# Eight GpSimd scatters moved two steps later in each turn of a selective-scan stage

## What is computed

```python
x = x + mamba(layernorm(x))      # per prompt: in_proj, conv, silu, delta, B, u
    # dA = exp(delta * -(n+1)), dBu = delta * u * B_n, 16 states n, 512 channels
    # h[t] = dA[t] * h[t-1] + dBu[t];  y[t] = sum_n h[t];  gate, out_proj
# routing of each prompt of the result:
e, p = top_k(softmax(layernorm(x) @ Wr), 2)
buf[e, b, pos] += x_rep          # every token is sent to its two experts' slots
```

## Time and profile before

| | |
|---|---|
| median of three runs | 3001.99 us (2996.59 to 3004.52) |
| profiled execution, its own time | 3004.03 us |
| its span, first to last instruction | 3002.2 us |
| mean granted TensorE clock | 0.968 |
| state-space stage, last scan begins | at 1601.8 us |
| a turn, from `last_send` to `last_send` (turns 3 to 15) | 97.2 to 98.1 us |
| the eight sends of a prompt, first to last start, turn 8 | 733.2 to 758.3 us |

### The profile page before, as it was taken

How to read it: one execution, slowest core, us unless ns; L and a number is a source line. 1 busy time by engine, 2 the same in 40 slices (tenths; PEclk the granted TensorE clock), 3 DMA queues, 4 the chain that set the end, 5 groups by cost and what they waited for, 6 DMA issues and landing times. The chain is left out here.

```text
span 3002.2 us, 48292 instructions
## 1 busy us (share of the span) xinstructions
PE 2777.6 (93%) x16944; PEld 2232.6 (74%) x16944; DVE 2243.1 (75%) x3482; ACT 1754.1 (58%) x3175; POOL 2216.2 (74%) x1565
## 2 busy tenths in 40 slices
PE   7899999999999999999976999999898986999998
PEld 3566666666566666666666999999777776999998
DVE  4999999989999999989886565656465554656564
ACT  5776777667766777677754454444445443545443
POOL 4889999999999999999996676664254446666664
PEclk9999999999999999999988999999999997999999
DMA  6222321132212321122122455553222223555552
GB/s 175 97 89 73 102 91 56 63 96 94 71 54 87 102 88 44 59 87 77 57 66 95 111 135 119 126 121 74 58 83 74 70 88 109 124 123 125 120 122 36
DMA packets 184204, 273.19 MB, mean 91 GB/s; under 512 B 35687, under 2 KB 156174, under 8 KB 175816
## 3 DMA queue, kind: packets, MB, share of 16 engines
q1 hardware_dynamic: 148680, 227.92, 24.1%
q0 software_dynamic: 35328, 42.76, 8.0%
HBM read 188.89 MB, written 94.72 MB: 94 GB/s over the span
## 5 line engine op out<-in xcount | busy, mean ns | idle before, releaser
L570 POOL TENSOR_TENSOR dbu<-du,bb 128x1024 f32<-128x1024 f32 x512 | 1195.8, 2362 | 21.9 <-DVE hs L730 16.6
L730 DVE TENSOR_TENSOR_SCAN hs<-da,dbu 128x1024 f32<-128x1024 f32 x512 | 1152.6, 2279 | 76.2 <-ACT da L665 34.5
L665 ACT ACTIVATE da<-delta 128x512 f32<-128x512 f32 x1024 | 568.1, 594 | 228.2 <-DVE hs L730 225.4
L835 PEld LDWEIGHTS yT<-ident,hs 128*128 128x128 f32 x4096 | 486.9, 146 | 138.0 <-issue 97.1
L835 PE MATMUL yT<-ident,hs 128*128 128x128 f32 x4096 | 543.8, 283 | 10.4 <-DVE hs L730 10.4
L1464 POOL TENSOR_TENSOR ffn_w_lo<-ffn_w,ffn_w_hi 128x512 fp32r<-128x512 f32 x240 | 319.9, 1350 | 78.0 <-ACT ffn_w_hi L1459 76.2
L1550 PE MATMUL ffn_hbank<-ffn_w_hi,ffn_hT_hi 128*128 128x256 f32 x1280 | 366.9, 287 | 1.6 <-DVE ffn_hT_lo L1537 1.6
L1552 PE MATMUL ffn_hbank<-ffn_w_hi,ffn_hT_lo 128*128 128x256 f32 x1280 | 361.2, 282 | 0.0
L1551 PE MATMUL ffn_hbank<-ffn_w_lo,ffn_hT_hi 128*128 128x256 f32 x1280 | 360.5, 282 | 0.0
L1515 PE MATMUL ffn_hbank<-ffn_rowsT_hi,ffn_w_hi 128*128 128x320 f32 x1024 | 318.6, 311 | 4.0 <-POOL ffn_w_lo L1464 3.3
L1516 PE MATMUL ffn_hbank<-ffn_rowsT_lo,ffn_w_hi 128*128 128x320 f32 x1024 | 318.1, 311 | 0.0
(11 more groups left out here) (279 smaller groups left out, 4966.4 us busy)
## 6 DMA issues: line engine op xcount, KB each, us to landing
bb<-b_rows SPq DMA_DIRECT2D x64, 1024.0 KB, 4.7
ffn_w<-L_ffn_W SPq DMA_DIRECT2D x60, 1024.0 KB, 8.8
slots<-empty SPq DMA_DIRECT2D x40, 530.0 KB, 7.4
empty<-slots SPq DMA_DIRECT2D x16, 662.5 KB, 5.0
ffn_rows<-slots SPq DMA_DIRECT2D x16, 662.5 KB, 4.9
xt<-L_attn_a_x SPq DMA_DIRECT2D x16, 512.0 KB
a_xn<-L_attn_a_x SPq DMA_DIRECT2D x16, 512.0 KB, 3.8
x_after_mamba<-a_xn SPq DMA_DIRECT2D x16, 512.0 KB
```

Of the source, the lines that this page charges most:

```text
L570: pool.tensor_tensor(dbu[:, s % DEEP], du[:, dt, :].unsqueeze(1).to_broadcast([P, SN, T]), bb[:, q * SN:(q + 1) * SN, :], ALU.mult).then_i ...
L665: ins = act.activation(da[:, s % 2, i, :], delta[:, par, dt, :], ACT.Exp, scale=-float(q * SN + i + 1))
L730: dve.tensor_tensor_scan(flat[0], flat[1], flat[2], 0.0, ALU.mult, ALU.add).then_inc(scanned.sem, 1)
L835: mm = pe.matmul(yT[:, j * P:(j + 1) * P], hs[:, s % DEEP, i, j * P:(j + 1) * P], k.ident[:], start=False, stop=(q == QS - 1 and i == SN - ...
```

## The change

The sends go behind the products of steps 3 to 10, where they stood behind those of steps 1 to 8. Nothing else is changed, and the lists of TensorE, VectorE, ScalarE and the DMA queue of SyncE are the same.

```diff
                     for s in range(STEPS):
                         if has_main(turn):
                             input_step(pool, turn - 1, s)
-                        if 1 <= s < 1 + NT * K and has_late(turn - 1):
-                            route_send(pool, r, turn - 3, s - 1)
+                        if 3 <= s < 3 + NT * K and has_late(turn - 1):
+                            route_send(pool, r, turn - 3, s - 3)
```

## The result

The changed kernel takes 3063.9 us (median of four runs, 3059.9 to 3069.6) where the kernel before, run beside it, takes 3002.2 us (2996.6 to 3004.5). The ratio is 1.0198, interval 1.0168 to 1.0228: 61.8 us slower. The forecast was 3064.8 us, range 3034 to 3090, and slower by over 0.3%.

The account below looks back on a forecast made before the run. Bound: TensorE's full stretch from 735.0 to 799 us and ScalarE's behind it. 41.8 us (holds net of order) plus 21 (clock) on 3004.0 gives 3066.8, less 2.0 for the median: 3064.8 us, range 3034 to 3090.

Parts of the forecast that it names:

- The order: GpSimd's later sends end TensorE's waits for hx (8.4 us in 13 turns) and turn 16's two waits: 11.0 us less.
- Turn 16's term: In turn 16, where TensorE isn't full, two waits of 1.28 us go whole: 2.6 us less.
- VectorE's wait for dbu at step 9: VectorE's scan of step 9 waits 1.29 us for GpSimd's product; this wait was to go.
- The holds: GpSimd's products of steps 2 and 3 delay VectorE's L262 to L269, so the first scan: 41.8 us net of the order.
- How the operations are held: L262, L264, L269 on VectorE each wait for a GpSimd product's end; the first scan starts 4.17 us later.
- The clock: TensorE's clock falls behind the new gap ahead of its full stretch: 1.5 us a turn, 21 us; bounds 0 and 47.
- No collision: Rival: VectorE's small operations get in between GpSimd's products, only the order counts: -11.0 us, 2991 us; chance 0.09.
- One product only: Rival: VectorE's chain runs through behind product 2: +9.3 us, with some lost clock 3010 to 3020 us; chance 0.07.
- The delay taken up by the wait for ysb: Rival: TensorE's later wait for ysb shrinks by 3.1 us a turn, so nothing is lost: about 3000 us; chance 0.03.

Follow-up runs that it names:

- run 1: The changed kernel, with GpSimd waiting for r_done ahead of the product of step 2: 2935.6 us, ratio 0.9965 to the kernel before.
- run 5: The changed kernel, with TensorE repeating its four uD matmuls seven times more ahead of step 0 in turns 3 to 16: 2988.5 us, ratio 1.0141 to the kernel before.
- run 4: The changed kernel without any edit, on a chip of the experiments: 3012.1 us, ratio 1.0224 to the kernel before.
- run 2: The changed kernel, with the sends behind the products of steps 2 to 9: 2980.7 us, ratio 1.0120 to the kernel before.

## Why the prediction was right

- **The order, −11.0 us.** Right in its sum, and run 1 alone measures it (−11.0). By that run's trace, against that of before from the first chip, turns 3 to 15 are 9.6 us shorter, where 8.4 was forecast, and turn 16 is 0.6 us shorter, where 2.6 was forecast, so the agreement to a tenth is luck. Turn 16's term failed because VectorE's waits there did not go whole: those for dbu fall from 2.6 us to 1.3 in run 1 and to nothing in the changed kernel, but those for da grow from 0.4 to 1.5 and 2.1. One step in the working was wrong as well: VectorE's wait for dbu at step 9 was to go, and in run 1 it only moves to step 11.
- **The holds, 41.8 us.** TensorE's new waits are 47.7 us in 13 turns and 3.96 in turn 16. Less the 8.4 for hx and the 2.6 forecast for turn 16 that is 40.7, and run 5, where the delay stands alone, gives 41.9 (40.1 by its stage). The first scan was to be 4.17 us late and TensorE 3.77: it waits 3.2 to 4.0.
- **How the operations are held.** The forecast had L262, L264 and L269 wait for the ends of products 1, 2 and 3, or L262 and L264 for those of 2 and 3. Seven turns go the first way and three the second. In four L262 is held for two products, which the forecast hadn't. The end is the same product, so no term changes. The port lock that the Trainium skill describes (SBUF — State Buffer, section Who interferes with whom) fits the rows of the change: copies and operations with two SBUF inputs are held (L262, L264 and L269: 0.36, 2.40 and 2.31 us), the scans with da in PSUM keep their 2.29 us. No run shows why a waiting L262 is sometimes passed over for a second product.
- **The clock, 21 us.** What is left of the stage's 66.0 us is 25.3, of which 5.7 stands in the two waits for uD, for which the forecast had no term; run 5 against run 4, which were made on two chips, gives 23.6. The value taken was 2.6 to 4.3 us short, within its bounds of 0 and 47. The value was picked between wide bounds because the gap is about as long as those of the other turns, and that reason doesn't hold: run 2 has as much of the loss with half the gap. That it came out close is in part luck.
- **The rivals.** No collision: excluded by the earlier trace rows against the chain of 5.6 us after. One product only: excluded in the change, and where it was made so (run 2) it costs 34 us, not the 8 to 18 that the rival was priced at, because of the clock. The delay taken up by the wait for ysb: excluded, since that wait is 52.1 us over the same 13 turns, as before.
- **The total.** 62.8 us were forecast, and the stage lost 66.0, the median 61.8. The two errors of the terms, −1.1 and +4.3, don't cancel. That the median hit within 1 us is luck: it needed some 4 us that the later layers, which the change doesn't touch, gave back (7.7 in the profiled pair).

## What to carry to other kernels

A wait that looks like idle time can be what keeps a chain on another engine short. Here 1.06 us of waiting by GpSimd, put back with one semaphore wait ahead of two products, is worth some 76 us. So before filling a gap, list what the other engines do in it, and whether such operations are held in the trace where the filler runs beside them. And a gap ahead of TensorE's full stretch is to be priced twice, for the time and for the clock behind it; matmuls that nobody needs can pay there.

## What was not expected

- An operation that meets a product may be held past its end and through the next one: L262 took 4.04 us while the product it met had 1.67 us to go (756.96 to 758.63). In run 4, the same kernel again, L262 once took 5.00 us.
- TensorE's clock cost 23.5 us with gaps of 1.5 to 2.0 us (run 2) and some 24 us with gaps of 3.2 to 4.0 (run 5 against run 4). In the changed kernel the eight matmuls of step 0 take 1.97 us in eight of the 14 turns, all with a wait of 3.8 to 4.0 us; in the others, with 3.2 to 3.6, they take 1.1 to 1.5, and the slow matmuls come behind them.
- The reduction L267, with one input, ran in its usual 0.21 us beside a product that held L269 for 2.31.
